# Deformable convolution, attention and LSTM on one core: offsets and Z on row halves of the array, a reordered sampling loop, own PSUM banks for the last turned E, fewer fills

## Chip, core and metric

One NeuronCore of a Trainium2 chip. The metric is device time in microseconds (us) of one execution; each engine (TensorE = PE, VectorE = DVE, ScalarE = ACT, GpSimdE = POOL, SyncE = SP for DMA) runs its own program in order and waits on semaphores.

## What is computed

Batch B = 4 images of 16 x 16 positions and C = 64 channels, all f32. The reference in short:

```python
g  = group_norm(x, 32)                                   # x: (4, 16, 16, 64)
om = conv3x3(g, offset_w) + offset_b                     # 27 numbers a position: 9 taps x (dy, dx), 9 masks
pos = clip(base + tap + offset, 0, 17)                   # where each tap samples
value = bilinear(pad(g), pos) * sigmoid(mask)            # 9 taps x 64 channels a position
x  = x + value @ dcn_w
t  = tokens(x)                                           # (4, 256, 64)
y  = layernorm(t)
t  = t + attention_block(y)                              # 8 heads of 32, softmax over 256 keys, gated FFN
t  = t + lstm_like(layernorm(t))                         # 256 steps in sequence, state 4 x 64
```

In the kernel bilinear sampling is a matrix product: for each tap, A[position, source] is the product of a hat in y and a hat in x (relu(1 - |pos - grid|)), and the sampled and weighted result is A turned (AT) times Z, where Z[source, tap] = g @ dcn_w[tap].

## The kernel before

Everything sits in SBUF after the first loads; there is one straight program for each engine, written out by Python loops, and the order on an engine is the order of the calls.

**Head.** PE runs fills (`fill`, bf16 matmuls of zeros whose result nobody reads) while x is loaded, one small matmul for the group norm, 8 fills more (`COLS_GROUPS` = 4096 columns), then the offset convolution: nine matmuls, one a tap, of 128 rows (two images above one another) by 54 outputs by 512 columns (both pairs of images). Even taps go to columns 0 to 53 of the array, odd taps to 64 to 117; ACT adds the bias to one half and DVE adds the other half (L806, L988). `z(i)`, 16 matmuls of 128 rows by 288 columns, makes Z; DW holds the weights with zeros in the rows of the other image. ACT copies each Z bank out (`z_out`). Four transposes turn the offsets (L433), from which ACT makes masks, DVE positions and distances, ACT the hats.

**Sampling loop.** 36 groups (image b, tap k), in 12 batches of `BATCH` = 3. DVE writes A (L1109), PE turns it (`turn`, four transposes of 128 x 128), ACT copies it (AT, L878), PE multiplies it by Z (`gather`, two matmuls of 128 rows x 64 outputs x 256 columns, L461). In batch j PE does `turn` of batch j, then `gather` of batch j - 1. The finished images' layer norm (`tokens`, `channels`), keys, queries and values stand in between at fixed batches (`TOKENS_AT`, `CHANNELS_AT`, `KEYS_AT`, `VALUES_AT`).

**First attention tile** (m = 0) runs before the first LSTM step: eight units u (half of the heads, image): `scores`, `exponents`, `turn_probs` (E transposed into a PSUM bank, L563), `turned` (ACT copy ET), `weigh` (L584), then DVE copies the heads O (L1125, L1132) and PE projects. Units 4 to 7 share two banks for the turned E. After it come FFN, two layer norms and the LSTM input (`turn_input`, L679), with fills on PE.

**LSTM.** 256 steps, each a chain PE L758 -> ACT -> DVE -> ACT -> DVE; attention tiles 1 to 7 and fills lie beside the steps. The functions of this part are the same in both kernels.

Tiles of the array: a matmul of up to 64 rows or up to 64 (32) outputs takes only a part of the 128 x 128 array, and its place follows from the partitions of its operands.

Of the kernel before, what the change touches and what calls it, by code (L numbers as in the profile page):

```python
# [42 lines left out]
HATS_AT = 3  # L43
BATCH = 3
TOKENS_AT = (4, 7, 10)
CHANNELS_AT = (5, 8, 11)
KEYS_AT = (4, 7, 10)
# [33 lines left out]
COLS_GROUPS = 4096  # L81
# [12 lines left out]
K_MASK = K_GRID + SIDE  # L94
K_END = K_MASK

CW_OW, CW_OB = 0, TAPS * OFFS2
# [12 lines left out]
def hybrid_kernel(nc, x_fm2, x_fm, conv_w, dcn_w, attn_w, lstm_w, vecs, consts, out):  # L110
    ctx = ExitStack()
    with ctx:
# [6 lines left out]
        def sem(name):  # L119
# [6 lines left out]
        DW = sb("DW", [P, 2, TAPS * C])  # L126
# [6 lines left out]
        base = K[:, K_BASE:K_GRID].rearrange("p (h k d) -> p h k d", h=2, d=2)  # L133
        grid = K[:, K_GRID:K_GRID + SIDE]
        OW = CW[:, CW_OW:CW_OB].rearrange("p (t o) -> p t o", t=TAPS)
        OB = CW[0:OFFS2, CW_OB:CW_OB + 1]
# [10 lines left out]
        OM = sb("OM", [OFFS2, 2, N])  # L147
        POS = sb("POS", [P, 2, B, TAPS, HALVES])
        MK = sb("MK", [P, B, TAPS, HALVES])
        HAT = sb("HAT", [P, 2, B, TAPS, HALVES, SIDE])  # L150
# [21 lines left out]
        ET = sb("ET", [P, 2, HALVES, P])  # L172
# [27 lines left out]
        b_misc, b_om, b_omt = banks[0], banks[1], banks[2]  # L200
        b_z = banks[3:8] + banks[0:1]
        b_at = banks[1:3] + banks[0:1]
# [7 lines left out]
        b_et_first, b_pv_first, b_pv_last = b_cs, b_c0, b_et  # L210

# [11 lines left out]
        om_mm, om_low, om_sb, omt_done, mask_act, dist, hat_abs, hat_act = (sem(n) for n in (  # L223
            "om_mm", "om_low", "om_sb", "omt_done", "mask_act", "dist", "hat_abs", "hat_act"))
# [164 lines left out]
        def _(pe):  # L389
# [18 lines left out]
            pe.wait_ge(xn_done, 2)  # L408

            for t in range(TAPS):  # L410
                dy, dx = t // 3, t % 3
                r = slice(C * (t % 2), C * (t % 2) + OFFS2)
                mm = nc.tensor.matmul(b_om[r, :].rearrange("p (j y x) -> p j y x", j=2, y=SIDE), OW[:, t, :],
                                      XN[:, :, dy:dy + SIDE, dx:dx + SIDE], start=(t < 2), stop=(t >= TAPS - 2))
            mm.then_inc(om_mm, 1)

            def z(i):
                b, pt = divmod(i, 2)
                if i >= 3:
                    pe.wait_ge(z_sb, 2 * (i - 2))  # L420
# [8 lines left out]
            for i in range(4):  # L429
                j, h = divmod(i, 2)  # L430
                if h == 0:
                    pe.wait_ge(om_sb, j + 1)
                mm = nc.tensor.transpose(b_omt[:, OFFS2 * i:OFFS2 * (i + 1)], OM[:, j, P * h:P * (h + 1)],  # L433
                                         ident[0:OFFS2, 0:OFFS2])
            mm.then_inc(omt_done, 1)
            for i in range(1, 2 * B):
                z(i)


            def turn(g):  # L440
                pe.wait_ge(a_done, g + 1)
                if g == 0:
                    pe.wait_ge(dist, 1)
                if g == 2:
                    pe.wait_ge(z_sb, 4 * B)
                elif g >= TURNS:
                    pe.wait_ge(at_sb, g - TURNS + 1)
# [7 lines left out]
            def gather(g):  # L455
                b, k = GROUPS[g]
                pe.wait_ge(at_sb, g + 1)
                if k == 0 and b >= 2:
                    pe.wait_ge(t0f_done, 2 * (b - 1))
# [5 lines left out]
            def tokens(b):  # L465

                pe.wait_ge(t0f_done, 2 * (b + 1))
                if b == 0:
                    pe.wait_ge(z_sb, 4 * B)
                else:  # L470
                    pe.wait_ge(yf_done, b)
# [77 lines left out]
            def turn_probs(m, u):  # L549
# [3 lines left out]
                elif m == 0 and i >= 5:  # L553
                    pe.wait_ge(et_sb, i - 1)
                    pe.wait_ge(e_inv, 4)
# [11 lines left out]
            def weigh(m, u):  # L567
# [9 lines left out]
                dst = b_pv if m else b_pv_last if b == B - 1 else b_pv_first  # L577
                if m == 0 and u == NU - HG:
                    pe.wait_ge(e_inv, NU - HG)
                for half in range(HALVES):  # L580
                    for h in range(HPG):
# [3 lines left out]
                                              V[:, b, half, c], ET[:, i % 2, half, TT * h:TT * (h + 1)],  # L585
# [3 lines left out]
            for j in range(len(GROUPS) // BATCH):  # L589
                for g in range(BATCH * j, BATCH * (j + 1)):  # L590
                    turn(g)
                if j in TOKENS_AT:
                    tokens(TOKENS_AT.index(j))
                if j in CHANNELS_AT[:-1]:
# [3 lines left out]
                if j >= 1:  # L598
                    for g in range(BATCH * (j - 1), BATCH * j):
                        gather(g)  # L600
                if j - 1 in KEYS_AT[:-1]:
                    keys_queries(KEYS_AT.index(j - 1))
# [27 lines left out]
            for u in range(4, NU):  # L630
                if u >= NU - 2:
                    fill(COLS_EARLY, b_x)
                turn_probs(0, u)
                weigh(0, u - 1)
            weigh(0, NU - 1)

            def project_turned(m, hg):

                pe.wait_ge(o_done, HG * m + hg + 1)
                if m == 0:  # L640
                    pe.wait_ge(o_early, HG)
# [121 lines left out]
            for g in EVERY:  # L763
# [15 lines left out]
                elif start(0) + PROJECT + 2 < g < start(0) + CELL_INPUT:  # L779
                    fill(COLS_EARLY if g < start(0) + NARROWED or g == start(0) + CELL_INPUT - 1 else MOST, b_cell[1])  # L780
# [3 lines left out]
        def _(act):  # L784
# [12 lines left out]
            def z_out(i):  # L797
                b, pt = divmod(i, 2)
                for m in range(2):
# [570 lines left out]
```

## Time and profile before

| | us |
|---|---|
| median of 3 runs | 384.88 (384.58, 384.88, 385.80) |
| the profiled execution, device time | 385.77 |
| its span, first to last instruction | 384.0 |
| from the span's start to the first LSTM step (L1284 at 87.44) | 87.44 |
| PE busy over the span | 364.0 (95%) |
| DVE, ACT, POOL busy | 239.1, 225.2, 56.5 |

A busy PE is not PE at its peak, since matmuls are pipelined and fills count as busy. What a change in the head is worth is read in the first 87 us, from the chain of work that ended last, not from these shares.

### The profile page before, as it was taken

What the parts mean: (1) busy time and instruction counts of PE and PEld (TensorE: products, weight loads), DVE (VectorE), ACT (ScalarE), POOL (GpSimd) and SP (SyncE); (2) the same over time, 40 slices, a digit from 0 to 9 for tenths busy, and PEclk for the clock granted to TensorE, in tenths of its full rate; (3) what the DMA queues carried; (4) which work ended last, traced back from release to release, by engine and by line L of the source; (5) the groups of instructions that cost most, each with busy time, mean ns of one, the idle gap of its engine ahead of it and who ended that gap; (6) DMA issues with size and microseconds to landing.
All of it is one profiled execution on the core that took longest, in us unless ns stands there. A gap on an engine that the chain in (4) does not pass through costs nothing.

```text
span 384.0 us, 15270 instructions
## 1 busy us (share of the span) xinstructions
PE 364.0 (95%) x5880; PEld 194.9 (51%) x5880; DVE 239.1 (62%) x1234; ACT 225.2 (59%) x1073; POOL 56.5 (15%) x124
## 2 busy tenths in 40 slices
PE   8999999899999999999999999999999999999996
PEld 2576765454554455445645554554455455543332
DVE  3388665645656666666666666757675666664443
ACT  2496664615854785477548655864686478544342
POOL 3101001311211220122011211211121112110000
PEclk9999999999999999999999999999999999999999
DMA  8000000000000000000000000000000000000000
GB/s 253 15 2 5 12 15 15 14 2 3 3 4 3 7 3 2 3 7 4 3 3 5 5 2 5 4 4 3 5 4 3 3 7 3 3 2 6 3 2 4
DMA packets 4806, 4.33 MB, mean 11 GB/s; under 512 B 3837, under 2 KB 4286, under 8 KB 4734
## 3 DMA queue, kind: packets, MB, share of 16 engines
q1 hardware_dynamic: 4432, 2.84, 2.7%
q8 instruction: 46, 0.75, 0.8%
q10 hardware_dynamic: 302, 0.52, 0.4%
q14 instruction: 26, 0.21, 0.2%
HBM read 2.57 MB, written 0.26 MB: 7 GB/s over the span
## 4 chain that ended last, share of the span: by engine, by line
PE 67%; DVE 15%; ACT 11%; issue 6%; DMA 1%; DVEq 0%; ACTq 0%
PE bank L758 18%; PE bank L394 12%; PE bank L546 9%; DVE bank L1290 6%; PE bank L563 5%; DVE H L1300 5%; ACT bank L934 4%; ACT bank L927 4%; PE bank L461 4%; PE bank L584 4%; PE bank L451 3%; PE bank L422 2%; ACT E L859 2%; PE bank L655 1%; PE bank L689 1%
## 5 line engine op out<-in xcount | busy, mean ns | idle before, releaser
L394 PE MATMUL bank<-FB 128*128 128x512 bf16 (+3 forms) x490 | 141.1, 369 | 1.2 <-DVE FB L956 1.2
L758 PEld LDWEIGHTS bank<-H,VW 64*32 64x32 f32 x3060 | 52.1, 106 | 104.9 <-DVE H L1300 103.1
L927 ACT ACTIVATE bank<-bank 64x8 f32<-64x8 f32 x256 | 37.6, 147 | 87.8 <-PE bank L758 84.6
L758 PE MATMUL bank<-H,VW 64*32 64x4 f32 x3060 | 74.3, 176 | 11.9 <-DVE H L1300 1.5
L1290 DVE TENSOR_TENSOR_SCAN bank<-bank,SU 64x12 f32<-64x12 f32 x256 | 48.5, 189 | 49.9 <-ACT bank L927 47.3
L1300 DVE SCALAR_TENSOR_TENSOR H<-TO,bank 64x4 f32<-64x4 f32 x256 | 40.7, 159 | 44.8 <-ACT bank L934 34.1
L394 PEld LDWEIGHTS bank<-FB 128*128 128x128 bf16 x490 | 38.7, 99 | 22.1 <-issue 4.2
L371 POOL TENSOR_SCALAR E<-E,rinv 128x256 f32<-128x256 f32 x62 | 29.8, 480 | 126.1 <-DVE rinv L1092 126.1
L934 ACT ACTIVATE bank<-bank 64x4 f32<-64x4 f32 x256 | 38.4, 150 | 15.9
L931 ACT ACTIVATE TO<-bank 64x4 f32<-64x4 f32 x256 | 43.8, 171 | 6.3
L1284 DVE SCALAR_TENSOR_TENSOR SU<-H,bank 64x4 f32<-64x4 f32 x256 | 41.2, 161 | 9.1
L546 PE MATMUL bank<-KF,QS 32*32 32x256 f32 x512 | 40.2, 386 | 0.0
L859 ACT ACTIVATE E<-bank,nmax 128x256 f32<-128x256 f32 x64 | 30.3, 474 | 2.6 <-DVE nmax L1083 1.1
L1075 DVE TENSOR_REDUCE nmax<-bank 128x1 f32<-128x256 f32 x64 | 27.1, 424 | 3.2 <-PE bank L546 1.4
L365 POOL TENSOR_TENSOR rs<-mv,half_neg 128x1 f32<-128x1 f32 x24 | 13.2, 550 | 102.8 <-DVE mv L1180 102.8
L563 PE MATMUL bank<-K,E 128*128 128x128 f32 x128 | 27.5, 296 | 0.4 <-DVE rinv L1092 0.4
L867 ACT COPY ET<-bank 128x256 f32<-128x256 f32 x64 | 23.8, 374 | 4.1 <-PE bank L563 2.6
L878 ACT COPY AT<-bank 128x512 f32<-128x512 f32 x36 | 19.1, 599 | 6.6 <-PE bank L451 6.6
L1109 DVE TENSOR_TENSOR A<-HAT 128x512 f32<-128x512 f32 x36 | 22.9, 680 | 0.1
L584 PE MATMUL bank<-ET,V 128*32 128x32 f32 x1024 | 21.3, 201 | 0.5 <-ACT ET L867 0.5
L451 PE MATMUL bank<-K,A 128*128 128x128 f32 x144 | 18.3, 277 | 0.0
L461 PE MATMUL bank<-AT,Z 128*64 128x256 f32 x144 | 18.2, 388 | 0.0
(123 smaller groups left out, 311.1 us busy)
## 6 DMA issues: line engine op xcount, KB each, us to landing
AW<-in_attn_w SPq DMA_DIRECT2D x1, 768.5 KB, 8.2
DW<-in_dcn_w SPq DMA_DIRECT2D x1, 576.0 KB, 6.7
X<-in_x_fm SPq DMA_DIRECT2D x1, 256.0 KB, 3.3
X<-in_x_fm ACTq DMA_DIRECT2D x1, 256.0 KB, 5.5
T<-T0T SPq DMA_DIRECT2D x16, 16.0 KB, 1.8
Y<-YT SPq DMA_DIRECT2D x16, 16.0 KB, 1.8
out_dram<-OUT SPq DMA_DIRECT2D x8, 32.0 KB, 1.4
CW<-in_conv_w SPq DMA_DIRECT2D x1, 243.5 KB, 4.0
```

The costliest lines, as they stand in the source:

```text
L394: nc.tensor.matmul(idle[:, 0:n], FB[:, 0:P], FB[:, 0:n], start=True, stop=True)
L546: mm = nc.tensor.matmul(score_bank(m, u)[r, 0:N], QS[r, hg, b, :], KF[r, hg, b, :], start=True, stop=True)
L563: mm = nc.tensor.transpose(turned_bank(m, u)[:, P * h:P * (h + 1)], E[:, i % UNIT_RING, P * h:P * (h + 1)], ident)
L584: mm = nc.tensor.matmul(dst[r, P * hg + TT * b:P * hg + TT * (b + 1)], V[:, b, half, c], ET[:, i % 2, half, TT * h:TT * (h + 1)], start=(h ...
L758: mm = nc.tensor.matmul(gate_out(m, gate, r, slice(B * s, B * (s + 1))), VW[0:C, gate, r], H[0:C, (STEPS * m + s - 1) % RING, :], start=Fa ...
L859: nc.scalar.activation(E[:, r, :], score_bank(m, u)[:, 0:N], ACT.Sigmoid, bias=nmax[:, r:r + 1], accum_out=sum_of(m, u)).then_inc(e_done, 1)
L927: nc.scalar.activation(GT[:, :, 1:3].rearrange("p b g -> p g b"), b_cell[m % 2][0:C, 0:2 * P].rearrange("p (g s b) -> p g s b", g=2, b=B)[ ...
L931: nc.scalar.activation(TO[:], gate_out(m, 2, slice(0, C), slice(B * s, B * (s + 1))), ACT.Tanh).then_inc(o_gate, 1)
L934: nc.scalar.activation(TC, CS[:, :, 2], ACT.Tanh, scale=0.5).then_inc(tanh_c, 1)
L1284: nc.vector.scalar_tensor_tensor(out=SU[:, :, 2], in0=H[0:C, (g - 1) % RING, :], scalar=0.5, in1=CS[:, :, 2], op0=ALU.mult, op1=ALU.mult). ...
L1290: nc.vector.tensor_tensor_scan(CS.rearrange("p b q -> p (b q)"), GT.rearrange("p b q -> p (b q)"), SU[:].rearrange("p b q -> p (b q)"), 0. ...
L1300: nc.vector.scalar_tensor_tensor(out=H[0:C, g % RING, :], in0=TO[:], scalar=1.0, in1=TC, op0=ALU.add, op1=ALU.mult).then_inc(h_done, 1)
```

## The change

- The offset convolution is done in two calls, `offsets(0)` and `offsets(1)`, one for each pair of images: 18 matmuls of 64 rows x 32 outputs x 256 columns each, on four places of the array (row half = image, column quarter = 2 x row half + tap parity), all into one bank. One ACT activation (pair 0) or one DVE instruction (pair 1) adds the bias; the four partial results are summed by the matmul that turns them (`partials`, a constant 0/1 matrix that makes K 54 columns wider).
- `z(i)`: two matmuls of 64 rows x 128 outputs x 288 columns, one for each image of a pair, into two banks. DW is half as large, CW is smaller. z(0) to z(3) (first pair) stand before the loop, z(4) to z(7) after the gathers of batches 1 to 4; their 16 copies on ACT are spread accordingly.
- Positions, masks and the hats of the first image are made in parts (taps 0 to 2 first, `SOONER`); pair 1 follows inside the loop.
- In the loop `channels` and `values` come after the gathers of their batch, and keys and queries move to `KEYS_AT` = (6, 9).
- `COLS_GROUPS` 4096 -> 2048: four fills in place of eight. One of the first tile's two late fills goes, and two of those shortly before the LSTM input (g = start(0) + 28).
- First tile: own banks for the turned E of units 5, 6 and 7 (`b_et_last`), a ring of four ET tiles, so that `turn_probs` 5, 6, 7 no longer wait for `turned`; heads are copied by image halves.

```diff
-COLS_GROUPS = 4096
+COLS_GROUPS = 2048
...
-            for t in range(TAPS):
-                dy, dx = t // 3, t % 3
-                r = slice(C * (t % 2), C * (t % 2) + OFFS2)
-                mm = nc.tensor.matmul(b_om[r, :].rearrange("p (j y x) -> p j y x", j=2, y=SIDE), OW[:, t, :],
-                                      XN[:, :, dy:dy + SIDE, dx:dx + SIDE], start=(t < 2), stop=(t >= TAPS - 2))
-            mm.then_inc(om_mm, 1)
+            def offsets(j):
+                pe.wait_ge(xn_done, j + 1)
+                for t in range(TAPS):
+                    dy, dx = t // 3, t % 3
+                    for h in range(2):
+                        r = slice(C * h, C * (h + 1))
+                        q = OM_TILE * (2 * h + t % 2)
+                        mm = nc.tensor.matmul(b_om[j][q:q + OM_TILE, 0:N].rearrange("p (y x) -> p y x", y=SIDE),
+                                              OW[r, t, :], XN[r, j, dy:dy + SIDE, dx:dx + SIDE],
+                                              start=(t < 2), stop=(t >= TAPS - 2))
+                mm.then_inc(om_mm, 1)
...
+                for h in range(HALVES):
+                    mm = nc.tensor.matmul(b_omt[j][:, OFFS2 * h:OFFS2 * (h + 1)], OM[:, j, P * h:P * (h + 1)], partials,
+                                          start=True, stop=True)
+                mm.then_inc(omt_done, 1)
...
-                for m in range(2):
-                    nc.tensor.matmul(b_z[2 * (i % 3) + m][:, 0:ZC],
-                                     XC[:, b // 2, P * pt:P * (pt + 1)], DW[:, b % 2, ZC * m:ZC * (m + 1)],
+                for h in range(2):
+                    r = slice(C * h, C * (h + 1))
+                    nc.tensor.matmul(b_z[i][h][:, 0:ZC], XC[r, j, P * pt:P * (pt + 1)], DW[r, ZC * m:ZC * (m + 1)],
                                      start=True, stop=True).then_inc(z_mm, 1)
...
+            offsets(0)
             z(0)
+            offsets_turned(0)
+            for i in range(1, 4):
                 z(i)
+            offsets(1)
...
+                if 1 <= j <= 4:
+                    z(3 + j)
...
-            return (b_et if m else b_s1 if u in (5, 7) else b_et_first)[:, 0:N]
+            return (b_et if m else b_et_last.get(u, b_et_first))[:, 0:N]
...
-            for u in range(4, NU):
-                if u >= NU - 2:
-                    fill(COLS_EARLY, b_x)
-                turn_probs(0, u)
-                weigh(0, u - 1)
-            weigh(0, NU - 1)
+            turn_probs(0, 4)
+            weigh(0, 3)
+            pe.wait_ge(e_inv, 5)
+            fill(COLS_EARLY, b_et_last[6])
+            turn_probs(0, 5)
+            turn_probs(0, 6)
+            weigh(0, 4)
+            turn_probs(0, 7)
+            weigh(0, 5)
+            weigh(0, 6)
+            weigh(0, 7)
...
-                    fill(COLS_EARLY if g < start(0) + NARROWED or g == start(0) + CELL_INPUT - 1 else MOST, b_cell[1])
+                    fill(COLS_EARLY if g < start(0) + NARROWED or g >= start(0) + CELL_INPUT - 2 else MOST, b_cell[1])
```

PE's order from the second set of fills to the third batch of the loop, before (L413 is the offset convolution, L433 the turned offsets, L422 Z, L451 `turn`, L461 `gather`; the last number counts matmuls):

```order
L394 MATMUL bank<-FB 128x512 x8
L413 MATMUL bank<-XN,CW 54x512 x9
L422 MATMUL bank<-DW,XC 128x288 x2
L433 MATMUL bank<-K,OM 128x54 x4
L422 MATMUL bank<-DW,XC 128x288 x14
L451 MATMUL bank<-K,A 128x128 x24
L461 MATMUL bank<-AT,Z 64x256 x6
L451 MATMUL bank<-K,A 128x128 x12
L461 MATMUL bank<-AT,Z 64x256 x6
```

The same stretch of PE's program in the changed kernel (L422 is now the convolution, L449 Z, L473 `turn`, L485 `gather`):

```order
L399 MATMUL bank<-FB 128x512 x4
L422 MATMUL bank<-XN,CW 32x256 x18
L449 MATMUL bank<-DW,XC 128x288 x2
L433 MATMUL bank<-K,OM 128x54 x2
L449 MATMUL bank<-DW,XC 128x288 x6
L422 MATMUL bank<-XN,CW 32x256 x18
L473 MATMUL bank<-K,A 128x128 x24
L433 MATMUL bank<-K,OM 128x54 x2
L485 MATMUL bank<-AT,Z 64x256 x6
L449 MATMUL bank<-DW,XC 128x288 x2
L473 MATMUL bank<-K,A 128x128 x12
L485 MATMUL bank<-AT,Z 64x256 x6
```

Half of the convolution and half of Z are ahead of the first `turn` as before; the second half of the convolution still is, the other half of Z is behind gathers, and the two matmuls that turn the second pair's offsets stand ahead of the first gather.

PE's order at the end of the first attention tile, from the turned E of unit 4 on, before (L563 `turn_probs`, L584 `weigh`, L394 a fill, each with the PSUM bank that it writes):

```order
L563 MATMUL bank2<-K,E 128x128 [waits e_norm,et_sb]
...
L563 MATMUL bank4<-K,E 128x128 [waits e_norm,e_inv,et_sb]
...
L394 MATMUL bank3<-FB 128x512
L563 MATMUL bank2<-K,E 128x128 [waits e_first,e_inv,et_sb]
...
L394 MATMUL bank3<-FB 128x512
L563 MATMUL bank4<-K,E 128x128 [waits e_first,e_inv,et_sb]
...
L584 MATMUL bank5<-ET,V 32x32 [waits e_inv,v_sb,et_sb]
```

The same place in the changed kernel (L586 `turn_probs`, L607 `weigh`, L399 a fill):

```order
L586 MATMUL bank2<-K,E 128x128 [waits e_norm,et_sb]
...
L399 MATMUL bank1<-FB 128x512 [waits e_inv]
L586 MATMUL bank4<-K,E 128x128 [waits e_norm,e_inv]
...
L586 MATMUL bank1<-K,E 128x128 [waits e_first,e_inv]
...
L607 MATMUL bank5<-ET,V 32x32 [waits e_inv,v_sb,et_sb]
...
L586 MATMUL bank3<-K,E 128x128 [waits e_first,e_inv]
```

The turned E of units 5, 6 and 7 have a bank each (4, 1, 3) and no longer wait for the copy of an earlier one (et_sb); one fill of two is gone, and only one `weigh` is left between the turned E of units 6 and 7.

## Rows read from the trace of the kernel before

**Rows 1.** Three stretches: busy us of each engine (instructions), granted clock, DMA share, GB/s.
```profile
0.00:9.67 9.67, 7.94 (x19) 2.65 (x20) 2.99 (x19) 1.99 (x3) 3.38 (x13) 1.00 0.84 254
22.72:63.40 40.68, 39.85 (x327) 28.00 (x327) 28.73 (x67) 26.54 (x58) 3.14 (x3) 1.00 0.05 11
87.44:384.00 296.56, 281.42 (x5195) 144.48 (x5195) 186.71 (x1070) 178.94 (x956) 42.36 (x91) 1.00 0.02 4
```

**Rows 2.** Chain that ended last, in order: start us, us, engine and line.
```profile
6.31 3.43 PE bank L394 x8
9.74 4.45 PE bank L413 x17
14.19 1.17 PE bank L422 x4
15.36 0.54 PE bank L433 x4
15.89 6.99 PE bank L422 x28
22.88 2.81 PE bank L451 x24
25.69 1.45 PE bank L461 x12
27.14 1.46 PE bank L451 x12
```

**Rows 3.** Timeline of the head: start us, us, engine, instructions, idle time before them.
```profile
7.88 0.74 DVE L982 TENSOR_SCALAR XN<-X,gmv,grs 128x256 f32<-128x256 f32 x2 [0.98 <-POOL grs L339]
...
11.02 0.13 PEld L413 LDWEIGHTS bank<-XN,CW 128*54 128x54 f32 x2 [0.30 <-issue]
...
14.23 0.83 ACT L806 ACTIVATE OM<-bank,CW 54x256 f32<-54x256 f32 x2 [4.81 <-PE bank L413]
...
16.48 0.77 DVE L999 TENSOR_TENSOR POS<-bank,K 128x18 f32<-128x18 f32 x8 [0.97 <-ACT MK L814]
...
20.38 1.89 DVE L1109 TENSOR_TENSOR A<-HAT 128x512 f32<-128x512 f32 x3
```

**Rows 4.** Timeline, matmuls on parts of the array (rows x outputs after the names).
```profile
39.81 0.70 PE L494 MATMUL bank<-YF,AW 64*128 64x256 f32 x4
...
64.57 1.06 PE L546 MATMUL bank<-KF,QS 32*32 32x256 f32 x16
```

**Rows 5.** Timeline, fills of the head and fills before the LSTM input.
```profile
6.17 3.57 PE L394 MATMUL bank<-FB 128*128 128x512 bf16 x8
...
84.61 1.69 PE L394 MATMUL bank<-FB 128*128 128x512 bf16 x7
```

**Rows 6.** Timeline, ACT's copies of Z and of AT.
```profile
19.76 3.56 ACT L801 COPY Z<-bank 128x288 f32<-128x288 f32 x10
...
27.76 1.56 ACT L878 COPY AT<-bank 128x512 f32<-128x512 f32 x3 [0.24 <-PE bank L451]
```

**Rows 7.** Timeline, end of the first attention tile.
```profile
76.21 0.35 DVE L1097 TENSOR_SCALAR E<-E,rinv 128x256 f32<-128x256 f32 x1
...
77.53 0.51 DVE L1125 COPY O<-bank 128x96 f32<-128x96 f32 x2 [0.97 <-PE bank L584]
77.62 0.38 PE L563 MATMUL bank<-K,E 128*128 128x128 f32 x2
...
78.04 0.37 ACT L867 COPY ET<-bank 128x256 f32<-128x256 f32 x1 [0.43 <-PE bank L563]
78.46 0.33 PE L584 MATMUL bank<-ET,V 128*32 128x32 f32 x16 [0.20 <-ACT ET L867]
78.93 0.27 DVE L1132 COPY O<-bank 128x64 f32<-128x64 f32 x1 [0.90 <-PE bank L584]
```

**Rows 8.** Timeline, the LSTM's first input.
```profile
86.14 0.31 DVE L1184 TENSOR_SCALAR LN<-T,mv,rs 128x64 f32<-128x64 f32 x1 [0.66 <-POOL rs L365]
...
86.79 0.30 PE L679 MATMUL bank<-K,LN 128*64 128x128 f32 x1
```

More of the change, by code:

```diff
@@ L43 @@
 HATS_AT = 3
+DISTANCES_AT = 1
+SOONER = 3
+OM_TILE = 32
 BATCH = 3
@@ L46 @@
 CHANNELS_AT = (5, 8, 11)
-KEYS_AT = (4, 7, 10)
+KEYS_AT = (6, 9)
 VALUES_AT = (6, 9)
@@ L593, in _ @@
                     tokens(TOKENS_AT.index(j))
+                if j in KEYS_AT:
+                    keys_queries(KEYS_AT.index(j))
+                if j == 1:
+                    offsets_turned(1)
+                if j >= 1:
+                    for g in range(BATCH * (j - 1), BATCH * j):
+                        gather(g)
+                if 1 <= j <= 4:
+                    z(3 + j)
                 if j in CHANNELS_AT[:-1]:
@@ L597, in _ @@
                     values(VALUES_AT.index(j))
[L598 to L602, printed above, removed]
             channels(2)
@@ L821, in hats_relu, with z_out @@
-            def hats_relu(b):
-                v = HAT[:, :, b, :, :, :].rearrange("p d k h v -> p d (k h v)")
-                act.wait_ge(hat_abs, b + 1)
-                nc.scalar.activation(v, v, ACT.Relu, bias=1.0, scale=-1.0).then_inc(hat_act, 1)
-            z_out(1)
-            z_out(2)
-            hats_abs(0)
-            hats_relu(0)
-            for i in range(3, 2 * B):
-                z_out(i)
+            def z_out(i, h):
+                j, pt, m = i // 4, i // 2 % 2, i % 2
+                act.wait_ge(z_mm, 2 * i + h + 1)
+                nc.scalar.copy(Z[:, pt, 2 * j + h, :, :].rearrange("p k f -> p (k f)")[:, ZC * m:ZC * (m + 1)],
+                               b_z[i][h][:, 0:ZC]).then_inc(z_sb, 1)
@@ new lines, in masks, with hats_abs @@
+            def masks(j):
+                act.wait_ge(pos_done, j + 1)
+                nc.scalar.activation(MK[:, j, :, :, :],
+                                     b_omt[j][:, 0:HALVES * OFFS2].rearrange("p (h b o) -> p h b o", h=HALVES, b=2)
+                                     [:, :, :, 2 * TAPS:OFFS], ACT.Tanh, scale=0.5).then_inc(mask_act, 1)
+            def hats_abs(b, taps, n):
+                v = HAT[:, b, :, taps, :, :].rearrange("p h k d v -> p h (k d v)")
+                act.wait_ge(dist, n)
+                nc.scalar.activation(v, v, ACT.Abs).then_inc(hat_abs, 1)
@@ new lines, in hats_relu @@
+            def hats_relu(b, taps, n):
+                v = HAT[:, b, :, taps, :, :].rearrange("p h k d v -> p h (k d v)")
+                act.wait_ge(hat_abs, n)
+                nc.scalar.activation(v, v, ACT.Relu, bias=1.0, scale=-1.0).then_inc(hat_act, 1)
+            act.wait_ge(ld_cw, 16)
+            act.wait_ge(om_mm, 1)
+            nc.scalar.activation(OM[:, 0, :], b_om[0][:, 0:N], ACT.Identity, bias=OB).then_inc(om_sb, 1)
+            z_out(0, 0)
+            z_out(0, 1)
+            masks(0)
@@ L880, in _ @@
                 j = g // BATCH
+                if j == 0 and g < 2:
+                    z_out(3, g)
+                elif 2 <= j <= 5 and g % BATCH < 2:
+                    z_out(2 + j, g % BATCH)
+                if g == 2 * BATCH - 1:
+                    masks(1)
                 if g % BATCH == BATCH - 1:
@@ new lines, in mask_scaled, with distances @@
+            def mask_scaled(j):
+                dve.wait_ge(mask_act, j + 1)
+                mk = MK[:, j, :, :, :].rearrange("p h b k -> p (h b k)")
+                link(nc.vector.tensor_scalar(mk, mk, 0.5, 0.5, ALU.mult, ALU.add))
+            def distances(b, taps):
+                pos = POS[:, b // 2, :, b % 2, 2 * taps.start:2 * taps.stop]
+                to = [P, HALVES, 2 * (taps.stop - taps.start), SIDE]
+                nc.vector.tensor_tensor(HAT[:, b, :, taps, :, :].rearrange("p h k d v -> p h (k d) v"),
+                                        pos[:, :, :, None].to_broadcast(to),
+                                        grid[:, None, None, :].to_broadcast(to), ALU.subtract).then_inc(dist, 1)
@@ L1021, in sampled, with masked @@
+            def masked(b, taps, n):
+                dve.wait_ge(hat_act, n)
+                v = HAT[:, b, :, taps, 0, :]
+                m = MK[:, b // 2, :, b % 2, taps]
+                link(nc.vector.tensor_tensor(v, v, m[:, :, :, None].to_broadcast([P, HALVES, taps.stop - taps.start, SIDE]),
+                                             ALU.mult))
             def sampled(b):
@@ L1316, in shape_constants @@
     k[:, K_GRID:K_GRID + SIDE] = np.arange(1, SIDE + 1)
+    for q in range(P // OM_TILE):
+        for o in range(OFFS):
+            k[OM_TILE * q + o, K_SUM + OFFS * (q // 2) + o] = 1.0
     return k
```

222 lines of the change are left out of this document (102 added, 120 removed).

## Prediction

> **What bounds the kernel now.** I read the stretches first, then the chain that ended last, then the timeline where the chain passes. The 296.6 us from the first LSTM step on [rows 1] are the recurrence, whose functions the change doesn't touch (the ring of four ET tiles only loosens a wait there). So the change is worth what it moves the first step's start, now 87.44 us.
>
> Of these 87 us the chain in the head is nearly all PE [rows 2]: fills until 9.7, the offset convolution 4.45, Z 1.17 + 6.99, the turned offsets 0.54, then turn and gather by turns. Z is 8.2 us that nothing hides, for PE works it off ahead of the first turn. In the loop PE is busy 39.85 of 40.68 us while DVE and ACT are at 28.7 and 26.5 [rows 1]: PE's sum sets the loop, and PE work that goes in or out counts in full.
>
> **What a matmul costs here.** L413's records lie 0.13 + 0.30 = 0.43 us apart [rows 3], for 512 columns: 0.84 ns a column. Nine f32 matmuls left 18 records, so each streams its columns twice. One after another that is 18 x 0.43 = 7.7 us, but it took 4.45 [rows 2]: even and odd taps, on different column halves, run side by side. Two row halves do as well: L494's four records of 256 columns (0.215 each, 0.86 in sequence) end within 0.70, about 0.43 and a pipeline's end. Four small places too: L546's 16 records, 3.4 us in sequence, end within 1.06 [rows 4]. In the loop 12 transposes stream 12 x 128 x 0.84 = 1.29 us and take 1.46, six gathers (12 records of 0.215, two column halves) 1.29 and take 1.45 [rows 2]: each switch between the kinds costs 0.16.
>
> **The clock.** The granted clock reads 1.00 in every stretch, the first one too [rows 1]. But the fills of the head lie 3.57 / 8 = 0.45 apart, later ones 1.69 / 7 = 0.24 [rows 5]: these are TensorE's two levels, 1.2 and 2.4 GHz, and the spacing is the better witness. The convolution's 0.84 ns a column is that of the loop, so the level rose at about 9.7, where the convolution begins, after 3.5 us of unbroken fills.
>
> **The change, term by term.**
>
> *Fills, 8 to 4.* They begin at 6.17 and end at 7.9 instead of 9.7. The next to be late is XN: the first of L982's two instructions ends near 8.3 [rows 3], and `offsets(0)` needs only that one. The convolution starts at 8.33 instead of 9.67.
>
> *Convolution.* 18 matmuls, four side by side: five rounds of two passes of 0.215, 2.15 us at the high level. If the level rises at 9.7 as now, the first 1.4 us do only 0.7 us of work: end at 8.33 + 2.15 + 0.7 + 0.16 = 11.3 instead of 14.19. Bounds: 10.6 with the high level throughout, 12.8 with the low one.
>
> *Bias, z(0), turned offsets.* ACT's bias takes 0.46 (two overlapping ones took 0.83 [rows 3]) beside z(0); DVE's addition after it is gone. z(0) to z(3) cost 2 x 288 x 0.84 = 0.48 each instead of 0.97, two row halves at once. With 0.6 for the two matmuls that turn and sum (bound: the four transposes' 0.54 [rows 2], and twice that), the offsets are turned at 12.5, z(3) is through at 14.1, and `offsets(1)`, 2.15 + 0.16, at 16.4. There the first turn begins; now the Z work before it ends at 22.88. DVE must have A by then: it took 3.9 us from the first POS (16.48) to the first A (20.38) [rows 3] for all four images; the new pieces are one image and three taps, so A starts near 14.5, and even at 3.9 us the first A would be 0.7 late.
>
> *To the first gather.* 24 transposes 2.81, then the second pair's turned offsets 0.5: 19.8 by PE's sum. But ACT now has two Z copies (3.56 / 10 = 0.36 each) among the first three AT copies (0.48 apart [rows 6]), and the sixth turn waits for the third AT copy, which lands near 19.3; with 0.6 for that turn and 0.5 for the offsets the gather begins at 20.5 instead of 25.69: **-5.2**, bound 19.8 from below.
>
> *Rest of the loop.* z(4) to z(7) go in: 4 x (0.48 + one more switch 0.16) = **+2.6**; bounds 1.9 (the switch hidden) and 3.2 (two switches each). ACT's ten late Z copies (3.6 us) come onto an engine with 14 us idle there. Channels behind the gathers and the later keys cost nothing: the same work, and token norms get more time. The offset and position work of pair 1 on DVE and ACT (under 2 us) hides the same way; if not, it is the loop's rival below.
>
> *End of the first tile.* E of unit 7 is ready at 76.21 + 0.35 = 76.56. Before it could be turned, the turned units 5 and 6, their copies and a fill had to pass, so that it was turned at 77.62 and the heads were done at 79.20 [rows 7]. With own banks the way is turn 0.38, copy 0.37, weigh 0.33, copy of 128 elements 0.39 (from 0.27 for 64 and 0.33 for 96), and 0.15 of hand-overs: 78.2. **-1.0**; bounds -0.5 (a copy queued ahead on ACT) and -1.2.
>
> *Before the LSTM.* LN is ready at 86.45, but L679 starts at 86.79 [rows 8], behind PE's fills and scores. Two fills less bring PE 0.48 earlier [rows 5]; then LN's 86.49 decides: **-0.3**.
>
> K grows by 54 columns and lands before x's statistics need it; CW and DW shrink. I take 0, +-0.1 for x's arrival.
>
> **Sum.** -5.2 + 2.6 - 1.0 - 0.3 = -3.9 on the profiled execution, 385.77 us with a span of 384.0: 381.9. The median of the runs shown is 384.88; one run is at 385.80 like the profile, two are 0.9 to 1.2 below. Should those be runs in which the level rose earlier (argued, not shown), their saving is smaller: the old convolution would start 1.3 earlier, the new one save only 0.7, so -3.3, and 381.6. Should it be something else, 381.0. I take **381.5**.
>
> **Rivals.**
>
> *The low clock lasts longer.* PE now pauses from 7.9 to 8.3, where it had no pause. If the level rises near 13, the convolution ends at 12.8, z(0) takes 0.3 more: +1.7, 383.2. For it speaks that the fills from 6.17 on still ran at the low level [rows 5], though nine other fills stand ahead of them; against it, that the convolution follows at once. The Trainium skill, "TensorE: Matmul & The Clock Gate", Part 1, says that the low level is the default, that activity lifts it, and that the moment varies from run to run; the spread of the three runs would agree, no run here shows it.
>
> *The four places don't run together.* All four of `offsets` write one bank from two row halves. If the halves take turns, each call lasts 4.3 instead of 2.15: +4.3, and 385.8, slower than before. This decides from 3.4 us lost (384.88 - 381.5), that is, when the two calls take over 7.7 us instead of 4.3. Against it: L546 ran four row groups into one score bank at the full rate [rows 4]. L494's two row halves have a bank each and don't tell. The Trainium skill, "TensorEngine Tiling (Array Packing)", Gotcha 1, says that different row tiles cannot access the same PSUM bank at the same time; by that rule the halves take turns and the time is this rival's 385.8, by L546's row the forecast's.
>
> *The loop gives more back.* Every in-order wait of ACT (Z copies between AT copies) or DVE (positions of pair 1) that PE feels costs some tenths in six batches: +1.5, 383.0. For it: the first batches are short of buffers (three banks); against it: 14 us of idle ACT.
>
> **Numbers.** Forecast 0.66, later clock 0.17, loop 0.08, tiles 0.09. Within 0.3% (1.15 us) is about what a measurement here can't tell from no change. The forecast, the later clock and the loop end mostly below 383.7: faster 0.85; the tiles' case gives same 0.09 and, with a low clock on top, slower 0.06 together with mishaps in the loop. Range: below, the hidden switches and ACT waits (0.7 + 0.7): 380.1; above, the later clock with double switches: 384.0.
>
> **What would show it.** The first convolution matmul near 8.3 and its 36 records over in 2.2 to 3 us; the first turn near 16.4; the first gather near 20.5; the last 2.6 earlier than now; heads done near 75.8; first step near 83.6. The steps after it must keep their spacing. Wrong would be: records of the upper and lower half in turn, fills' spacing of 0.43 carried into z(0), or gathers of batches 1 to 4 more than 3.7 apart.

## Result and profile after

| | before | after |
|---|---|---|
| median, us (20 executions each) | 384.56 | 382.85 |
| lowest, highest | 384.49, 385.84 | 381.54, 384.48 |
| the profiled execution, its span | 385.77, 384.0 | 384.46, 382.6 |

The ratio is 0.995, 95% interval 0.9938 to 0.9962: faster by 1.7 us, half of the 3.4 forecast, with a median inside the range (380.1 to 384.0), whose upper end was drawn from the first rival. The kernel before lies in two groups, 16 executions at 384.5 to 384.9 and 4 at 385.6 to 385.84; the changed kernel is spread over 3 us. (Executions disturbed by a clock that fell for tens of microseconds are left out of every median and comparison; the profiled ones of two experiments, eight fills and halves in turn, were such from 86 us on, and only rows ahead of that are read.)

The windows of the changed kernel, in the columns of [rows 1]: up to the convolution, in its first call, in the loop, from the first step on.

```profile
0.00:8.80 8.80, 6.31 (x15) 2.04 (x15) 2.77 (x19) 1.28 (x1) 3.11 (x12) 1.00 0.77 230
8.84:12.90 4.06, 4.06 (x36) 1.96 (x36) 0.17 (x1) 0.71 (x2) 2.02 (x6) 1.00 0.12 42
...
22.83:63.00 40.17, 39.18 (x319) 26.63 (x318) 27.97 (x66) 25.56 (x59) 3.14 (x3) 1.00 0.05 11
86.04:382.60 296.56, 273.42 (x5145) 144.46 (x5195) 186.83 (x1070) 178.94 (x956) 42.44 (x91) 1.00 0.02 4
```

The recurrence takes as long as before (296.56 in both windows, whose ends are known to a tenth), so the whole change is in where the first step starts. The chain of the changed kernel (start, us, what), which answers to [rows 2]:

```profile
0.72 3.67 DMA X<-in_x_fm
...
8.84 4.37 PE bank L422 x36
...
21.26 1.26 PE bank L473 x8
...
22.90 1.45 PE bank L485 x12
24.35 0.69 PE bank L449 x4
...
34.22 0.31 ACT Z L833
...
34.67 0.31 PE bank L497 x2
34.98 1.45 PE bank L485 x12
...
61.59 1.47 PE bank L485 x12
```

The convolution (L422) takes 4.37, nearly as long as the old one, where 2.97 was forecast. The first gather (L485) starts at 22.90, 2.8 earlier than in [rows 2], not 5.2. The timeline says why; it answers to [rows 3, 5]:

```profile
6.57 1.87 PE L399 MATMUL bank<-FB 128*128 128x512 bf16 x4
...
8.28 0.73 DVE L1023 TENSOR_SCALAR XN<-X,gmv,grs 128x256 f32<-128x256 f32 x2 [0.98 <-POOL grs L344]
8.84 4.37 PE L422 MATMUL bank<-XN,CW 64*32 64x256 f32 x36 [0.40 <-DVE XN L1023]
...
10.09 0.23 PEld L422 LDWEIGHTS bank<-XN,CW 64*32 64x32 f32 x4 [0.20 <-issue]
10.52 0.23 PEld L422 LDWEIGHTS bank<-XN,CW 64*32 64x32 f32 x4 [0.20 <-issue]
...
16.07 2.35 PE L422 MATMUL bank<-XN,CW 64*32 64x256 f32 x36
18.35 1.53 PE L473 MATMUL bank<-K,A 128*128 128x128 f32 x12
18.86 0.75 DVE L1055 TENSOR_TENSOR HAT<-POS,K 128x576 f32<-128x576 f32 x1
20.13 0.48 DVE L1033 TENSOR_SCALAR OM<-bank,CW 128x256 f32<-128x256 f32 x1
20.27 0.66 PE L473 MATMUL bank<-K,A 128*128 128x128 f32 x4 [0.39 <-DVE A L1167]
21.26 1.26 PE L473 MATMUL bank<-K,A 128*128 128x128 f32 x8 [0.34 <-DVE A L1167]
```

In `offsets(0)` four weight loads, one for each place, come every 0.43 us. That is one pass of 256 columns at the low level of the clock (1.2 GHz), twice the 0.215 that the prediction reads from [rows 4], though the granted clock reads 1.00 there. `offsets(1)`, the same work, takes 2.35. So the level rose only at the end of the first call, near 13, and not at 9.7 as in the trace of before. And turns 4 and 5 wait for A, since `distances(1)` (L1055) and `offsets_out` (L1033) stand between the A's on DVE. The end of the tile and the LSTM's input, answering to [rows 7, 8]:

```profile
75.92 0.35 DVE L1143 TENSOR_SCALAR E<-E,rinv 128x256 f32<-128x256 f32 x1
...
76.42 0.44 PE L586 MATMUL bank<-K,E 128*128 128x128 f32 x2
...
77.79 0.29 DVE L1183 COPY O<-bank 128x128 f32<-128x128 f32 x1 [1.31 <-PE bank L607]
...
83.49 1.25 PE L399 MATMUL bank<-FB 128*128 128x512 bf16 x5
85.02 0.31 DVE L1234 TENSOR_SCALAR LN<-T,mv,rs 128x64 f32<-128x64 f32 x1 [0.66 <-POOL rs L370]
85.39 0.30 PE L711 MATMUL bank<-K,LN 128*64 128x128 f32 x1
```

E of unit 7 is ready at 76.27 and turned from 76.42 on: 0.15 after it was ready, where it was 1.06 in [rows 7]. LN is ready at 85.33 and turned at 85.39. The stages of the two profiled executions, before and after: to the start of the first gather 25.69 and 22.90 (-2.79); to the last gathers, 61.88 and 61.59, so 36.19 and 38.69 (+2.50); to the end of the heads' copy 17.33 and 16.50 (-0.83); to the first step, 87.46 and 86.06, 8.25 and 7.97 (-0.28). Sum -1.40, against -3.9.

The +2.50 of the loop is a sum of its own. From the first to the last gathers PE is busy 37.70 instead of 35.36 us, +2.34: the four pairs of Z cost 0.69 each, 2.76, and other work on PE 0.42 less. Its idle time goes from 0.83 to 0.99. Before, it was two waits for the first images' normed tokens (YT), which the changed kernel no longer has:

```profile
38.00 0.44 PE L480 MATMUL bank<-K,YT 128*128 128x128 f32 x2 [0.42 <-DVE YT L1045]
...
49.24 0.44 PE L480 MATMUL bank<-K,YT 128*128 128x128 f32 x2 [0.41 <-DVE YT L1045]
```

Now it is one wait of 0.99 ahead of L497, the turned tokens of the first image: its bank is free only when ACT has copied a late piece of Z, which stands behind a copy of AT in ACT's queue (34.22 in the chain above).

### The profile page after: what moved, and what is told of

Same layout as the page of the kernel before. It is cut to its first block, busy times and chain, and to the rows that moved or that the text cites. A ratio compares the mean times of both kernels' runs of the same rounds, so it can differ in the third digit from the quotient of the medians.

```text
span 382.6 us, 15322 instructions
## 1 busy us (share of the span) xinstructions
PE 352.9 (92%) x5878; PEld 193.0 (50%) x5931; DVE 238.8 (62%) x1230; ACT 224.6 (59%) x1072; POOL 56.6 (15%) x124
## 4 chain that ended last, share of the span: by engine, by line
PE 64%; DVE 15%; ACT 12%; issue 7%; DMA 1%; POOL 0%; DVEq 0%; ACTq 0%; POOLq 0%
PE bank L790 18%; PE bank L399 9%; PE bank L570 8%; DVE bank L1340 6%; PE bank L586 5%; DVE H L1350 5%; PE bank L485 5%; ACT bank L975 4%; ACT bank L968 4%; PE bank L473 4%; PE bank L607 4%; ACT E L894 2%; PE bank L687 1%; PE bank L721 1%; PE bank L422 1%
## 5 line engine op out<-in xcount | busy, mean ns | idle before, releaser
L399 PE MATMUL bank<-FB 128*128 128x512 bf16 (+3 forms) x430 | 126.1, 364 | 9.0 <-issue 7.8
L399 PEld LDWEIGHTS bank<-FB 128*128 128x128 bf16 x483 | 37.8, 98 | 20.7 <-issue 3.1
L586 PE MATMUL bank<-K,E 128*128 128x128 f32 x128 | 27.6, 297 | 0.5 <-DVE rinv L1138 0.4
L913 ACT COPY AT<-bank 128x512 f32<-128x512 f32 x36 | 20.3, 602 | 8.7 <-PE bank L473 8.6
L607 PE MATMUL bank<-ET,V 128*32 128x32 f32 x1024 | 21.0, 201 | 0.1
L473 PE MATMUL bank<-K,A 128*128 128x128 f32 x144 | 18.6, 277 | 0.7 <-DVE A L1167 0.7
L485 PE MATMUL bank<-AT,Z 128*64 128x256 f32 x144 | 18.2, 388 | 0.0
```

Source lines behind the costliest of these rows:

```text
L399: nc.tensor.matmul(idle[:, 0:n], FB[:, 0:P], FB[:, 0:n], start=True, stop=True)
L485: mm = nc.tensor.matmul(b_cv[b % 2][C * pt:C * (pt + 1), 0:N], Z[:, pt, b, k, :], AT[:, g % SLOTS, pt, :, :], start=(k == 0), stop=(k == T ...
L586: mm = nc.tensor.transpose(turned_bank(m, u)[:, P * h:P * (h + 1)], E[:, i % UNIT_RING, P * h:P * (h + 1)], ident)
```

## Experiments

Theory A: the pause ahead of the convolution lets TensorE's clock rise late, or fall again; the rest of the change does what was forecast. Theory B: the clock doesn't depend on the fills; they only stand in the way. "11 fills" below is the changed kernel with this edit:

```diff
-COLS_LOAD = 4608
+COLS_LOAD = 5632
```

The stations of each profiled execution, from its chain (us from the span's start; length of `offsets(0)` or of the old convolution):

| | convolution | its length | first gather | last gathers | heads copied | first step |
|---|---|---|---|---|---|---|
| before | 9.74 | 4.45 | 25.69 | 61.88 | 79.21 | 87.46 |
| before, 11 fills | 8.65 | 4.48 | 24.63 | 60.83 | 78.16 | 86.41 |
| after | 8.84 | 4.37 | 22.90 | 61.59 | 78.09 | 86.06 |
| after, once more | 8.16 | 4.04 | 21.89 | 60.59 | 77.08 | 85.06 |
| after, 11 fills | 8.18 | 2.35 | 20.22 | 58.91 | 75.42 | 83.39 |
| 11 fills, A sooner, mended | 8.09 | 2.35 | 19.22 | 58.49 | 74.99 | 82.97 |

**Eight fills again** (`COLS_GROUPS` 2048 -> 4096 in the changed kernel).

> The changed kernel with the eight fills of before ahead of the convolution. Theory A (the pause between four fills and the convolution lets the low clock last into the convolution): without the pause the convolution starts later (8.5 to 10) but runs in 2.3 to 2.6 us instead of 4.37, so that the first turn is no later than 18.4 and the time 382.0 to 383.0, with less spread between executions than the 3 us of the changed kernel. Theory B (the clock rises when it does whatever PE is given; the fills only stand in the way): the convolution starts 1.3 later and ends later too, 384.1.

382.46, ratio 0.9928 (0.9906 to 0.995), five executions at 382.09 to 382.54 and one at 383.95. The time is A's, not B's:

```profile
5.98 1.89 PE L399 MATMUL bank<-FB 128*128 128x512 bf16 x8
8.24 2.35 PE L422 MATMUL bank<-XN,CW 64*32 64x256 f32 x36 [0.37 <-DVE XN L1023]
```

At the high level eight fills take 1.89 and are through before XN is, so four fewer gain nothing. But this execution doesn't show that the eight fills raised the level: its first nine took 3.54 instead of 4.02, so it was up before them.

**Four fills in the kernel before** (`COLS_GROUPS` 4096 -> 2048 there).

> The kernel before with four fills instead of eight and nothing else, so with the old convolution of 54 outputs and 512 columns. Theory A: the pause does it whatever the convolution's form, the 18 passes lie 0.43 apart on each half and more (4.45 becomes 6 or more), and the time is 384.5 to 386, no gain. Theory A2 (it is the convolution on small places that keeps the clock low): here the clock rises as in the kernel before, the convolution starts 1.3 earlier, and the time is 383.2 to 384.0. Theory B gives 383.3 too, with the convolution's length unchanged.

387.14 against 385.12, ratio 1.0035 (1.0018 to 1.0052): this one edit alone makes the old kernel slower. B falls, and so does the thought that the small places keep the clock low, since the old kernel suffers as well. Six of twelve executions lost 2.2 to 2.5 us, more than expected, and four 1.3 to 1.8; the profiled one was one of two that lost nothing (385.16, convolution 4.47 at 8.58). So the longer convolution (6 or more) that A expected is in no trace; for it speak the times and, in the four, a mean granted clock of 0.994.

**11 fills** (edit above).

> The changed kernel with 11 instead of 9 fills at the start, so that PE is busy from 1.2 up to the group norm's matmul near 6.1; four fills follow as in the changed kernel. Theory A: the level rises ahead of the convolution in nearly all executions, the convolution takes 2.3 to 2.6 us, the first turn starts near 16.5, and the time is 381.5 with a spread of about 1 us. Theory B: 382.85 as the changed kernel, or up to 0.3 more where the fills are in the way of the group norm's matmul.

382.37, ratio 0.993 (0.9906 to 0.9955). In the timeline PE was busy up to the group norm's matmul, and `offsets(0)` ran at the high level from its first record:

```profile
1.17 4.56 PE L399 MATMUL bank<-FB 128*128 128x512 bf16 x11 [1.17 <-DVE FB L997]
5.70 0.36 PE L408 MATMUL bank<-gme,K 128*128 128x4 f32 x2
5.92 1.02 PE L399 MATMUL bank<-FB 128*128 128x512 bf16 x4
8.18 2.35 PE L422 MATMUL bank<-XN,CW 64*32 64x256 f32 x36 [1.24 <-DVE XN L1023]
```

The pause is still there, 1.24 long. Four executions lie at 382.14 to 382.47, one at 384.53 (mean granted clock 0.993). The level of 381.5 is missed because this chip's recurrence takes 0.5 longer: 380.4 - 83.39 = 297.0, against 296.5 (four fills in the kernel before and Z twice, on the same chip, have 296.9 and 297.0); the first step is where it was forecast (83.6).

**Z in the loop twice.**

```diff
+                for h in range(2 if i >= 4 else 0):
+                    r = slice(C * h, C * (h + 1))
+                    nc.tensor.matmul(b_z[i][h][:, 0:ZC], XC[r, j, P * pt:P * (pt + 1)], DW[r, ZC * m:ZC * (m + 1)],
+                                     start=True, stop=True)
```

> The changed kernel with each of the four Z pairs that stand in the loop (z(4) to z(7)) computed twice into the same banks; only the second pair reports. Theory A (PE sets the loop, so PE work in it counts in full): four more pairs of 0.48, 1.9 us more, 384.8. Rival (after the change the loop waits for ACT or DVE and hides PE work): less than 0.6 more, 383.4 at most.

385.23, ratio 0.9992 (0.9977 to 1.0007). In its chain the doubled pair stands in the path at 0.48, the first at 0.69 with the switch of kinds:

```profile
21.01 1.45 PE bank L489 x12
22.46 0.69 PE bank L449 x4
23.14 0.48 PE bank L453 x4
...
61.65 1.47 PE bank L489 x12
```

From first to last gathers 40.64 instead of 38.69: +1.95 for 4 x 0.48. PE sets the loop. In this execution the clock rose inside the convolution, as the forecast had it; it ran from 8.39 to 11.32 (forecast 8.33 to 11.3):

```profile
8.39 2.93 PE L422 MATMUL bank<-XN,CW 64*32 64x256 f32 x36 [0.43 <-DVE XN L1027]
```

**Late fills back**, on 11 fills.

```diff
-                    fill(COLS_EARLY if g < start(0) + NARROWED or g >= start(0) + CELL_INPUT - 2 else MOST, b_cell[1])
+                    fill(COLS_EARLY if g < start(0) + NARROWED or g == start(0) + CELL_INPUT - 1 else MOST, b_cell[1])
```

> The changed kernel with 11 fills at the start (as the run before with that edit, whose first LSTM step started at 83.39), and one of the two fills groups shortly before the LSTM input back to its old length (three fills instead of one at one place). Theory (PE's queue was what LN's turn waited for): turn_input starts 0.3 to 0.4 after LN is ready instead of at once, the stretch from the heads' copy to the first step is 8.25 instead of 7.97, and the time 0.3 longer. Rival (LN was late for another reason): stretch and time unchanged within 0.1.

382.2, ratio 0.9918 (0.9899 to 0.9937). Its timeline:

```profile
80.60 1.69 PE L399 MATMUL bank<-FB 128*128 128x512 bf16 x7
...
82.13 0.31 DVE L1234 TENSOR_SCALAR LN<-T,mv,rs 128x64 f32<-128x64 f32 x1 [0.66 <-POOL rs L370]
...
82.78 0.30 PE L711 MATMUL bank<-K,LN 128*64 128x128 f32 x1
```

LN is ready at 82.44 and waits 0.34. From heads (75.20) to first step (83.45) 8.25: +0.28, as before the change. Against the run with 11 fills the time can't be compared to 0.3, since that ran on the slower chip.

**Old end of the first tile**, on 11 fills: banks, order, ring of two ET tiles and copies of before. The core of the edit:

```diff
-            return (b_et if m else b_et_last.get(u, b_et_first))[:, 0:N]
+            return (b_et if m else b_s1 if u in (5, 7) else b_et_first)[:, 0:N]
```

> The changed kernel with 11 fills at the start and with the end of the first attention tile as in the kernel before: two banks for the turned E of units 4 to 7, two ET tiles, the old order with two fills, heads copied as before. Theory: all that this part of the change gave comes back, 0.8 more from the last gathers to the heads' copy (17.33 instead of 16.50), and 0.8 more time. Rival (the earlier heads are swallowed by the layer norms and fills behind them): the stretch grows by 0.8, the time by less than 0.3.

383.5, ratio 0.9956 (0.9939 to 0.9973). Last gathers at 58.97, heads copied at 76.30: 17.33, +0.82, and it arrives whole at the first step (84.28). The time rose more, by 1.3 against the run with late fills on the same chip (the profiled spans by 1.9), where 0.82 less that run's own 0.28 was due. Another 1.0 of the profiled execution is lost within the steps (381.8 - 84.28 = 297.5 instead of 296.5). One step of its chain that is late, where DVE's H starts 0.23 after ACT without a wait that the profile shows, is this:

```profile
278.94 0.16 ACT bank L971
279.09 0.23 issue
279.33 0.17 DVE H L1354
```

What makes it late stays open; the kernel before, with the same ring of two, doesn't show it (296.5).

**A sooner**, on 11 fills: the part of the edit on DVE. On PE the second pair's turned offsets go behind the first gathers, on ACT its masks and the hats of image 1 come later.

```diff
-                if g == SOONER:
+                if g == 2 * SOONER:
                     distances(1, slice(0, TAPS))
-                elif g == SOONER + 1:
                     offsets_out()
-                elif g == 2 * SOONER:
+                elif g == 2 * SOONER + 2:
                     positions(1)
```

> The changed kernel with 11 fills at the start, and on DVE the distances of image 1 and the bias of the second pair moved from between the fourth and fifth A behind the sixth; the second pair's turned offsets come after the first gathers, its masks and the hats of image 1 later. Theory (the turns of the second batch wait for A because of these two DVE instructions): turns 4 to 6 wait at most for ACT's copies, the first gather starts near 19.0 instead of 20.2, the first Z pair behind it 0.6 to 0.8 sooner, since the turned offsets (0.5) only change place, and the time is 0.6 to 0.8 less than with 11 fills alone, 381.7 on a chip where the kernel before takes 385.1. Rival (the loop's sum on PE and the AT copies take it back, or the hats of image 1 come too late for the fourth batch): no gain, or up to 1 more.

382.97, ratio 0.9939 (0.9919 to 0.9958): the rival's result. The first gather came at 19.24 instead of 20.22. About half of that are the turned offsets, which only change place; the rest is the wait for A. But the loop then took 40.79 instead of 38.69. DVE's timeline shows two new waits ahead of image 1:

```profile
24.09 0.46 DVE L1064 TENSOR_TENSOR HAT<-HAT,MK 128x288 f32<-128x288 f32 x1 [1.58 <-ACT HAT L851]
25.03 0.18 DVE L1049 TENSOR_SCALAR MK<-MK 128x36 f32<-128x36 f32 x1 [0.49 <-ACT MK L839]
```

ACT had the second hat activation and the masks queued behind copies of AT and Z that waited for PE.

**Halves in turn**, on 11 fills: all nine taps of one row half, then of the other.

```diff
-                for t in range(TAPS):
-                    dy, dx = t // 3, t % 3
-                    for h in range(2):
+                for h in range(2):
+                    for t in range(TAPS):
+                        dy, dx = t // 3, t % 3
```

> The changed kernel with 11 fills at the start, and the 18 matmuls of each call of the convolution in another order: first the nine taps of the one row half, then those of the other, instead of by turns. The work is the same. If the four places run together because neighbours in PE's queue go to different places: each call takes 4.3 instead of 2.3, 2.0 more twice, and the time is 4 more, 386.3. If PE lets later matmuls run past waiting ones: no difference. If the row halves could not use one bank at the same time anyway: no difference either, but then the order by turns would not have taken 2.35.

383.80, ratio 0.9963 (0.995 to 0.9976), where 386.3 was expected. The order counts, but less than I had:

```profile
8.39 3.65 PE L422 MATMUL bank<-XN,CW 64*32 64x256 f32 x36 [1.19 <-DVE XN L1023]
```

3.65 instead of 2.35. The last tap of the one half and the first of the other still make a pair, so nine pairs of two passes of 0.215, 3.87 at most; my 4.3 counted five rounds for each half. So in this bank the places run together as far as neighbours in the queue have different ones.

**A sooner, mended.** The second hat activation directly behind the first, masks one AT copy sooner, their scaling two groups later. The edit against A sooner:

```diff
-                if k == (HATS_AT + 2 if b else 7) and b + 1 < B:
+                if k == (HATS_AT + 2 if b else 6) and b + 1 < B:
...
-                if g == 2 * BATCH + 1:
+                if g == 2 * BATCH:
                     masks(1)
...
-                elif g == TAPS:
+                elif g == TAPS + 2:
                     mask_scaled(1)
```

> As the run with A sooner, but the second hat activation of image 1 directly behind the first, the second pair's masks one ACT copy of AT earlier, and their scaling on DVE two groups later, so that none of them stands in front of work that PE waits for. Theory (the loss after the first gather came from these waits in line): first gather near 19.2, the loop from first gather to last 39.3 instead of 40.8 (38.7 and the 0.58 of the turned offsets that moved into it), first step 0.3 to 0.5 earlier than with 11 fills alone (83.4), the time 0.4 less than that, 381.8 where the kernel before takes 385.0. Rival (the loop loses again elsewhere): no better than with 11 fills alone, 382.3.

381.53 against 384.84, ratio 0.991 (0.9896 to 0.9925), all executions within 0.54 us: the lowest median of all, 0.3 to 0.4 below the early executions of the changed kernel on the same chip (381.82 to 381.90, below). From 19.22 to 58.49 the loop takes 39.27, as expected.

**The kernel before with 11 fills** (the same edit there).

> The kernel before with 11 fills at the start and nothing else. Theory (the two levels of times of the kernel before, 1.2 apart, are executions with the clock rising ahead of the second set of fills or only behind it; the profile on which the prediction was summed was one of the late ones): all executions now lie with the lower group, the convolution starts at 8.6 instead of 9.7, the first gather at 24.6, first step at 86.3, and the median is that of the lower group of the kernel before on the same chip or at most 0.1 above. Rival (the groups come from something else): two groups 1.2 apart as before.

384.85, ratio 0.9996 (0.9987 to 1.0005), all twelve between 384.71 and 385.13; the upper group, in which 11 of the 33 executions of the kernel before on this chip lie (385.6 to 386.14), is gone. Its chain:

```profile
8.65 4.48 PE bank L413 x18
...
24.63 1.45 PE bank L461 x12
```

So the two groups are an early and a late rise, 1.06 apart at the first gather, and the profile of before was of the late kind.

**The changed kernel once more.**

> The changed kernel itself, unaltered, on the chip of the two other runs of this call. Theory (its nine fills and the pause leave the moment of the rise to chance): times spread over 2 to 3 us again, from 2.7 below the lower group of the kernel before to 0.2 below it, median 1.5 to 2.2 below the median of the kernel before. Rival (the spread belonged to the other chip): spread under 1 us.

Three executions at 381.82 to 381.90, two at 383.33 and 383.44; ratio 0.9928 (0.9906 to 0.9949). The spread of 1.6 is less than expected, and the median, 381.90, is 2.9 below the kernel before instead of 1.5 to 2.2: of five executions three were early ones. The profiled one is of the second kind. Its windows over the pause, the convolution and after (columns as in [rows 1]):

```profile
5.90:8.10 2.20, 1.02 (x6) 0.28 (x5) 0.99 (x5) 0.00 (x0) 0.88 (x2) 1.00 1.06 325
8.36:11.76 3.40, 3.40 (x34) 2.08 (x28) 0.16 (x1) 0.71 (x2) 1.68 (x5) 0.50 0.16 58
11.80:15.00 3.20, 3.20 (x24) 1.90 (x20) 1.35 (x5) 2.15 (x7) 0.00 (x0) 1.00 0.00 0
```

The same stretch in its timeline:

```profile
5.90 1.02 PE L399 MATMUL bank<-FB 128*128 128x512 bf16 x4
8.16 4.04 PE L422 MATMUL bank<-XN,CW 64*32 64x256 f32 x36 [1.24 <-DVE XN L1023]
```

Here the level had risen in time (four fills in 1.02), PE then idled 1.24, the granted clock fell to 0.50 as the convolution began and came back near 11.8. This is the second half of A in one trace. That the pause is the cause, one trace can't show, for the pause of the run with 11 fills was as long; the mean granted clocks on record speak for it. They are 0.993 to 0.995 in 14 of the 48 executions with nine fills and then four (of either kernel), in one of the 33 with 11 and then four, and in none of the 74 with eight in second place.

For the first half, the late rise, the second set of fills tells: it ran at the high level in all seven profiled executions with 11 fills ahead (1.02 to 1.07 for four, 1.89 for eight), but in three of the six with nine (the others: 1.87 for four, 3.57 for eight). With nine, PE stood idle 0.47 to 1.04 between them and the group norm's matmul; with 11 it did not. A rise that comes late falls on fills that nobody waits for when there are eight (3.57, then the convolution at the high level in 4.45), and on the convolution when there are four (1.87, then 4.37). That the short pause ahead of the convolution delays the rise isn't shown: it was 0.40 in the changed kernel's profile, with the rise near 13, and 0.43 in that of Z twice, with the rise inside the convolution.

The 20 executions of the changed kernel can be sorted by time and mean granted clock. Each kind has one profile, of this kernel or a variant, that fits; the sorting itself is argued.

| executions | us | mean clock | rise of the level | profile that fits, its first gather |
|---|---|---|---|---|
| 5 | 381.54 to 381.75 | 1.000 | early | 11 fills, 20.22 |
| 7 | 382.44 to 382.95 | 1.000 | inside the convolution | Z twice, 21.01 |
| 5 | 383.23 to 383.85 | 0.994 | early, then taken back | once more, 21.89 |
| 3 | 384.09 to 384.48 | 0.999 | at the convolution's end | the changed kernel, 22.90 |

## Why the forecast was half right

- *Fills, 8 to 4* ("The convolution starts at 8.33"): it starts at 7.97 to 8.39 in the nine other profiled executions of the changed kernel and its variants, at 8.84 in the profile, where x landed 0.40 later (3.67 instead of 3.27). That isn't the larger K, for the run with eight fills has it too, and x landed in 3.28.
- *Convolution* ("if the level rises at 9.7 as now"): **this is the step that failed**. With the rise inside the convolution, 2.93 measured against 2.97; but the rise isn't a date that four fills fewer leave alone. It came ahead of the convolution, in it, or behind it, or was taken back by the pause, and the length went from 2.35 to 4.37. By the sorting above the first rival (chance 0.17, 383.2) came true in 8 of 20 executions, and the median is of the second kind, with the convolution as forecast. But the 381.5 also needs the rise to be as early as in the kernel before: 16 of its 20 executions have that, and only 5 of the changed kernel's. My argument against the rival, that the convolution follows at once, doesn't hold: in the profile PE idled only the 0.40 that was counted on, and the rise came near 13; in the last experiment it idled 1.24. The Trainium skill, "TensorE: Matmul & The Clock Gate", Part 1, says that the moment varies from run to run; the traces agree, and show 2 to 3 us on the whole kernel's time for it.
- *To the first gather*: 4.1 forecast from the first turn, 4.55 measured with either clock, since turns 4 and 5 wait for A (0.4 mis-sized; the bound by PE's sum, 16.4 + 2.81 + 0.5, is 19.7 and not 19.8). The two edits that put A sooner bear it out: 0.42 at the first step (82.97 against 83.39).
- *Rest of the loop* +2.6: +2.50, but by luck in part. "Channels behind the gathers and the later keys cost nothing": they gave back the 0.83 of waits for YT. The ten late Z copies on ACT were to hide: one cost a wait of 0.99. That is the loop's rival (+1.5) at work, once, and its sign, gathers more than 3.7 apart, shows at that place (30.09 to 34.98); another wait of its kind is the one for A ahead of the first gather. Its sum didn't come, since the two waits before were gone.
- *End of the tile* -1.0: -0.83, and +0.82 undone. *Before the LSTM* -0.3: -0.28, and +0.28 undone. Both are shown at the first step; in the time of whole executions neither was measured alone.
- *Four places*: 36 records in 2.35 into one bank from two row halves, at the rate of [rows 4], so that rival is out; the rule of the Trainium skill, "TensorEngine Tiling (Array Packing)", Gotcha 1, doesn't hold for these rows.
- *The sum's base*: the profile of before was of its slower group. The prediction had priced this ("level rose earlier", 381.6), with 1.3 for the old kernel's gain from an early rise, which is 1.06 at the first gather. With the clock up in both kernels, 11 fills each (on two chips, whose heads run alike from the convolution on), the terms are -4.41 to the first gather, +2.49, -0.82, -0.28: -3.02 at the first step (86.41 to 83.39). 384.56 - 3.0 gives 381.6, where the fastest quarter of the changed kernel lies. The median execution lost another 1.2 (382.85 - 381.6), by the sorting above to the clock.

## What to carry to other kernels

Here the fills ahead of the first heavy work weren't a delay to be cut by their length: once the clock was up they cost nothing that showed (385.16 with four, 384.9 to 385.2 with eight, in the kernel before), and a pause in the place of four of them (0.9 to 1.7 us) cost up to 2.5. A term that comes out right can be two errors that cancel: look at the waits in it. Look at the spread of the executions and at which group the profiled one is from before a sum is made against it. An instruction put "where the engine is free" needs a look at what stands behind it in that in-order queue: two on DVE cost 0.45, and moving them without their followers on ACT cost 1.5 (40.79 against 39.27).

## What the hardware showed unexpectedly

- The granted clock fell from 1.00 to 0.50 near 8.36, behind a pause of 1.24 us, and cost 1.7 us of convolution. With 11 fills ahead the same pause left it up in the profiled execution, and the mean granted clock is 0.997 or more in 32 of 33.
- Pairs on different row halves and column places ran together from one bank (2.35 for 36 records), but only as far as the queue's order put them beside each other (3.65).
- The statistics on x, which wait for its landing, start between 3.70 us (halves in turn) and 4.42 us (changed kernel) with the same loads, a difference larger than the smaller terms of the sum.
